# Local attention's output leaves PSUM by a ScalarE copy and is divided by the softmax sums on GpSimd, instead of one VectorE product on the way out

## What is computed

```python
# attention of one layer, 16 heads of 64, windows of 32 tokens that also see the window before
q, k, v = split(shift_tokens(x) @ Wqkv)
q, k = rotary(l2norm(q) * q_scale), rotary(l2norm(k) * k_scale)
attn = softmax(where(mask, -big, 8.0 * q @ k.T))     # per window: 32 queries by 64 keys
x = (attn @ v) @ Wo + x
# feed-forward of one layer
xn = layernorm(shift_tokens(x)) * g + b
a, gate = split(xn @ W1 + b1)
x = (a * gelu(gate)) @ W2 + b2 + x
```

## Time and profile before

| | us |
|---|---|
| median of 3 runs (4414.82 to 4419.62) | 4414.89 |
| the profiled execution, its own time | 4412.12 |
| its span in the trace | 4410.3 |
| busy: TensorE (PE) matmuls | 3768.9 (85%) |
| busy: VectorE (DVE) | 3571.7 (81%) |
| busy: GpSimd (POOL) | 2895.4 (66%) |
| busy: ScalarE (ACT) | 2656.4 (60%) |

### The profile page before, as it was taken

How to read it: one execution, slowest core, us unless ns; L and a number is a source line. 1 busy time by engine, 2 the same in 40 slices (tenths; PEclk the granted TensorE clock), 3 DMA queues, 4 the chain that set the end, 5 groups by cost and what they waited for, 6 DMA issues and landing times. The chain is left out here.

```text
span 4410.3 us, 109941 instructions
## 1 busy us (share of the span) xinstructions
PE 3768.9 (85%) x41516; PEld 2856.2 (65%) x41516; DVE 3571.7 (81%) x5298; ACT 2656.4 (60%) x4035; POOL 2895.4 (66%) x2520
## 2 busy tenths in 40 slices
PE   5666666669999899998999989999899999899996
PEld 3444444357777777776777767777677777677774
DVE  6777777678888788887888878888888888888884
ACT  5666666546666566656566656656566656566663
POOL 3555555357777677676767666777677676667672
PEclk9888888889999999999999999999999999999998
DMA  1111111032222322223222232222322222222221
GB/s 38 53 53 53 53 53 45 8 90 64 55 60 56 92 59 62 56 58 91 62 55 62 56 88 65 55 58 54 89 60 67 56 56 78 70 60 63 56 55 58
DMA packets 157205, 267.21 MB, mean 61 GB/s; under 512 B 32062, under 2 KB 51644, under 8 KB 152380
## 3 DMA queue, kind: packets, MB, share of 16 engines
q1 hardware_dynamic: 157116, 266.19, 22.1%
HBM read 44.81 MB, written 26.21 MB: 16 GB/s over the span
## 5 line engine op out<-in xcount | busy, mean ns | idle before, releaser
L789 POOL TENSOR_TENSOR st_qk_rot<-st_qk_rot,st_qk_sq 128x1024 f32<-128x1024 f32 x384 | 920.4, 2397 | 939.6 <-DVE st_qk_sq L686 939.6
L429 PE MATMUL st_ps<-st_wqkv,st_xs 128*128 128x512 f32 x3456 | 956.7, 412 | 66.2 <-DMA st_wqkv<-wqkv_parts 37.7
L537 ACT ACTIVATE st_qk_sq<-st_ps 128x1024 f32<-128x1024 f32 x384 | 393.9, 1026 | 652.6 <-PE st_ps L429 652.0
L429 PEld LDWEIGHTS st_ps<-st_wqkv,st_xs 128*128 128x128 f32 x3456 | 612.4, 190 | 231.4 <-issue 97.8
L809 POOL TENSOR_TENSOR st_qk_rot<-st_qk_rot,st_rn 128x1024 f32<-128x1024 f32 x384 | 722.7, 1903 | 15.0
L1426 POOL TENSOR_TENSOR at_probs<-at_probs,at_rden 128x128 f32<-128x128 f32 (+3 forms) x512 | 361.8, 738 | 389.6 <-DVE at_rden L1357 389.6
L668 DVE TENSOR_REDUCE st_nt<-st_qk_sq 128x16 f32<-128x1024 f32 x384 | 465.7, 1213 | 175.5 <-ACT st_qk_sq L537 175.4
L686 DVE TENSOR_TENSOR st_qk_sq<-st_ps,st_rot 128x512 f32<-128x512 f32 x768 | 490.2, 678 | 0.0
L672 DVE TENSOR_TENSOR st_qk_rot<-st_ps,st_rot 128x1024 f32<-128x1024 f32 x384 | 465.9, 1213 | 8.6 <-PE st_ps L444 8.6
L444 PE MATMUL st_ps<-consts_sb,st_qk_rot 128*128 128x128 f32 x3072 | 403.0, 274 | 27.9 <-DVE st_hid L769 16.5
L437 PEld LDWEIGHTS st_ps<-st_oT,st_wo 128*128 128x128 f32 x3072 | 368.8, 192 | 79.4 <-issue 75.8
(11 more groups left out here) (125 smaller groups left out, 6828.4 us busy)
## 6 DMA issues: line engine op xcount, KB each, us to landing
st_v_bd<-st_v_tok SPq DMA_DIRECT2D x1152, 128.0 KB, 2.3
st_v_bd<-st_v_tok SPq DMA_DIRECT2D x672, 64.0 KB, 2.1
wqkv_parts<-at_w_parts SPq DMA_DIRECT2D x18, 1024.0 KB, 4.5
st_wqkv<-wqkv_parts SPq DMA_DIRECT2D x18, 1024.0 KB, 5.7
at_w_raw<-in_wqkv SPq DMA_DIRECT2D x18, 512.0 KB, 4.1
rotary_tables<-at_rot SPq DMA_DIRECT2D x6, 512.0 KB, 2.8
st_rot<-rotary_tables SPq DMA_DIRECT2D x24, 128.0 KB, 2.4
st_wo<-in_wo SPq DMA_DIRECT2D x6, 512.0 KB, 4.2
```

Source lines behind the costliest of these rows:

```text
L429: last = pe.matmul(out[:, c * 512:(c + 1) * 512], xs[:, x_part, t * P:(t + 1) * P], rhs, start=(n == 0), stop=(n == len(PASSES) - 1))
L537: act.activation(qk_sq[:, cols_of(a)], slot_of("qk"[a], 0, t), ACT.Square).then_inc(squared[a], 1)
L789: pool.tensor_tensor(qk_rot[:, cols], qk_rot[:, cols], qk_sq[:, cols], ALU.add).then_inc(rot_done[a], 1)
```

## The change

The product L759 leaves VectorE. In its place ScalarE copies o out of PSUM into `st_o` unchanged, as the first thing of the next step, ahead of the square of q, and raises `taken["o"]`. GpSimd then multiplies `st_o` in place by the reciprocals and raises a new semaphore, `o_scaled`; in step 1 this stands behind the four products of the layer norm's Newton chain, in every step ahead of the rotation's additions. The ot job waits for `o_scaled` instead of `taken["o"]`. VectorE waits for `o_scaled` of two tiles before ahead of the sums L749, so that it doesn't overwrite the reciprocals.

```diff
@@ jobs of TensorE
                             elif kind == "ot":
-                                pe.wait_ge(taken["o"], tiles_done(u, d, index))
+                                pe.wait_ge(o_scaled, tiles_done(u, d, index))
@@ ScalarE, first in a step
+                        if alive(u, d3):
+                            act.wait_ge(ready["o"], 2 + (n - 3))
+                            if not (start and n < 5):
+                                act.wait_ge(ready["ot"], n - 4)
+                            act.activation(o[:, :], slot_of("o", d2, t2), ACT.Copy).then_inc(taken["o"], 1)
                         if alive(u, 0):
                             square(0)
@@ VectorE, late in a step
                             dve.wait_ge(exp_ready, n - 2)
+                            if not (start and n < 5):
+                                dve.wait_ge(o_scaled, n - 4)
                             dve.tensor_reduce(den[:, t2 % 2, 0, :], s[:, t2 % 2, :].rearrange("p (h k) -> p h k", h=HEADS),
                                               AX.X, ALU.add).then_inc(den_ready, 1)
                             dve.wait_ge(den_ready, 2 * (n - 2) - 1)
                             dve.reciprocal(den[:, t2 % 2, 1, :], den[:, t2 % 2, 0, :]).then_inc(den_ready, 1)
-                        if alive(u, d2):
-                            dve.wait_ge(ready["o"], n)
-                            dve.wait_ge(den_ready, 2 * (n - 2))
-                            if not (start and n < 4):
-                                dve.wait_ge(ready["ot"], n - 3)
-                            dve.tensor_tensor(
-                                o[:, :].rearrange("p (h d) -> p h d", h=HEADS),
-                                slot_of("o", d2, t2).rearrange("p (h d) -> p h d", h=HEADS),
-                                den[:, t2 % 2, 1, :].unsqueeze(2).to_broadcast([P, HEADS, DH]),
-                                ALU.mult).then_inc(taken["o"], 1)
@@ GpSimd, behind the Newton chain of step 1, ahead of the rotation
                             pool.tensor_tensor(xc[:, :], xc[:, :], xc2[:, :], ALU.mult).then_inc(ff_newton, 1)
+                        d, tt = divmod(t - 3, TILES)
+                        if alive(u, d):
+                            pool.wait_ge(taken["o"], n - 3)
+                            pool.wait_ge(den_ready, 2 * (n - 3))
+                            by_head = o[:, :].rearrange("p (h d) -> p h d", h=HEADS)
+                            pool.tensor_tensor(by_head, by_head, den[:, tt % 2, 1, :].unsqueeze(2).to_broadcast([P, HEADS, DH]),
+                                               ALU.mult).then_inc(o_scaled, 1)
                         if alive(u, 0):
                             rotate(0)
```

More of the change, by code:

```diff
@@ L243, in local_stack @@
         ff_gain, ff_newton, pool_own = sem("ff_gain"), sem("ff_newton"), sem("pool_own")
+        o_scaled = sem("o_scaled")
         def jobs_of(t):
```

## The result

The changed kernel takes 4713.51 us (median of 4 runs, 4703.46 to 4717.46) against 4414.85, a ratio of 1.0676 with an interval of 1.0651 to 1.0701. Forecast were 4702 us.

The account below looks back on a forecast made before the run. TensorE's nearly unbroken row of jobs was taken to bound the kernel. 47 x (3.3 + 2.0 + 0.8) = 287 us on 4412.1 gave 4699, and 2.8 us for the median 4702; range 4600 to 4755.

Parts of the forecast that it names:

- VectorE's product goes, and in steps 3, 0 and 2 this is worth nothing: VectorE, steps 3, 0 and 2: 1.23 us less per tile only lengthens its wait for ScalarE's square; worth nothing.
- The copy costs nothing in steps 3, 0 and 1: ScalarE, steps 3, 0 and 1: the 1.02 us copy lies within the 1.5 us q job; cost nothing.
- 0.8 us in step 2: ScalarE, step 2: copy between table load and square of q delays exponential and pt; 0.8 us per turn, 0.6 to 1.0.
- GpSimd's product costs nothing in steps 3, 0 and 2: GpSimd, steps 3, 0 and 2: the 1.90 us product fits idle time ahead of its additions; cost nothing.
- ot in step 1 waits for it until 11.1 us, 3.3 us later: Step 1: GpSimd's product stands behind the Newton chain, so ot starts late; 3.3 us per turn, 3.2 to 4.0.
- The clock falls and costs 2.0 us: TensorE, step 1: 4.9 us idle ahead of ot drops the clock to 0.50; 2.0 us per turn, nothing to 2.25.
- pt, scores, z, o and the hidden products follow without a wait: TensorE, step 1 behind ot: the whole row of jobs moves with ot; GpSimd's end, some 0.7 us later, delays nobody.
- The sum: All turns: 47 x (3.3 + 2.0 + 0.8) = 287 us on the profiled execution's 4412.1.
- the clock holds: Rival, step 1: no clock fall behind the idle stretch; 47 x 4.1 = 193 us, 4608 us; chance 0.13.
- The chain was not held up: Rival, step 1: VectorE's instructions get between GpSimd's chain, 0.74 us more, clock may cost 2.25; 4748 us; chance 0.11.
- VectorE's relief: Rival, step 1: bank wait shrinks by 1.23 us if scaled o is there by 2547.6; 56 us faster, 4359; chance 0.03.
- The rule of the Trainium skill: TensorE's clock ramp, under 1% of a typical span: all turns would pay at most 44 us, giving 4652; not followed.

Follow-up runs that it names:

- the run with the load alone: Kernel before, VectorE's product kept, plus one GpSimd product of the same shape at the new one's place, on a tile nobody reads: 4432.48 us, 1.0043.
- the two runs with the moved instruction: Layer norm's last VectorE instruction moved ahead of the mask of the scores in step 1: in the kernel before 4401.58 us, in the changed kernel 4692.16.
- the version with both moves: Changed kernel with GpSimd's product ahead of the Newton chain in step 1 and ScalarE's copy of o ahead of the GELUs: 4444.51 us, 1.0067.

## Why the prediction was right

The number, 4702 against 4713.5, came out of the right steps, with small errors of size that partly cancel.

- *VectorE's product goes, and in steps 3, 0 and 2 this is worth nothing.* Right: 15.81 and 15.96 us for steps 3 and 0, before and after.
- *The copy costs nothing in steps 3, 0 and 1.* Right. *0.8 us in step 2*: 0.62. The copy takes 0.92 us of ScalarE's row, start to start, not 1.02, and more idle time ahead of the square of k was used up than the 0.22 counted. The run with the early copy gives all of it back.
- *GpSimd's product costs nothing in steps 3, 0 and 2.* Right, by the lengths of steps 3 and 0 (step 2's loss is the copy's), and by the run with the load alone.
- *ot in step 1 waits for it until 11.1 us, 3.3 us later.* Right: 11.21, 3.4 us later, 3.0 at the five changes of layer, 3.34 in the mean; moving the product ahead of the chain takes it away.
- *The clock falls and costs 2.0 us.* The mechanism was right, and so was the mean: 1.9 to 2.25 us by filling the stretch, 2.04 by the two runs with the moved instruction. That the mean came out so well is in part luck. The prediction expected the same cost in every turn, at most 2.25 us. The 46 turns paid different amounts: from ot to the end of step 1 takes 2.97 us longer than before in the 28 long turns, some 2.7 of it without the longer wait for the layer norm, and 1.1 us longer in the turns of 25.4. How many turns are of which kind no row of the kernel before could tell.
- *pt, scores, z, o and the hidden products follow without a wait.* This is the step that failed, though for little: the hidden products wait 0.3 to 0.7 us in 28 turns. The wait of 0.24 us that most turns had before goes off against it, so that some 0.2 us per turn remain. GpSimd's later end was taken as harmless because no job waits for it; but VectorE's last layer norm instruction, now behind late scores, meets GpSimd's L807 and holds up the hidden products. Rows 3 had shown L656 held up in the same way, and the prediction named it only ahead of the chain.
- *The sum*: 3.3 + 2.0 + 0.2 + 0.6 = 6.1 us per turn as forecast, with 0.2 for the layer norm in the place of 0.2 too much for the copy; by the starts of q it is 284 / 46 = 6.2 in the profiled execution. The sum counted 47 turns; the last of them has no new tiles and lies in the 7 us outside the 46.
- *The rivals.* That the clock holds is out by the granted clock. The chain was not held up: L663 did get in ahead of L843, which then took 2.35 us, but L814 took 1.03 instead of 1.49, and the chain ended 9.2 us into the step against 9.1. VectorE's relief is real, about 15 us, but only where o is there in time and nothing takes its place; as the change stood it could not be had, as the rival's own condition said. It is also less than the 1.2 us per turn of the rival: step 1 goes from 20.55 to 20.07 us, since pt, which could start 1.3 us sooner, then waits for the exponential and starts 0.6 sooner.
- *The rule of the Trainium skill ("TensorE: Matmul & The Clock Gate", Part 1) that the clock's ramp costs under 1% of a span and needn't be fitted* would have given 4652. The clock's share was 85 us or more, near 2% of the time, so it does not hold for this kernel, in which the ramp is paid in each turn of a loop.

## What to carry to other kernels

An operation that is moved to an engine with room on average takes the place in line that it is given there: look up, in the one step in which that engine is full, what stands ahead of it, and move it ahead of work that is due later. When TensorE gets a new wait in each turn of a loop, look at the granted clock behind it and count the slower work as well as the wait: here 2.0 us behind 3.3 us of delay. When a wait is removed, ask what is late next: here it was an instruction of 0.5 us, held five times as long by another engine's work. Moving it was worth 12 us in the kernel before and 57 us in the version with both moves, more than the whole relief that the change was about.

## What the runs showed that was not expected

- With 40 more pairs of TensorE instructions in the loop's body the instruction queue moved 7.09 instead of 0.59 MB, and 44 turns had some 3.8 us of waiting more, 41 of them with a fall of the clock behind it. Eight more pairs did not. Where between them the bound lies was not tried.
- Behind 2.47 us of idle time the clock fell in ten turns and not in 30 others, in the same kernel at the same place; behind the changed kernel's 3.2 and 5.0 us it fell in every turn, behind 3.5 to 4.5 us in the run with 40 transposes in 41 of 44. The length of the idle time alone does not tell.
- The changed kernel's step 1 has three lengths, 27.3, 25.4 and 23.8 us, and how often each comes depends on the length of the other steps: a move that saved 0.62 us in step 2 saved 0.51 in step 1 as well, where TensorE's order and the start of ot stayed as they were.
